# Layer-0 edge messages: VectorE's order of work, gathers by four tiles, and the sum of message parts

## The reference

```
x0, x1 = up0[snd], up1[snd]
m0e = tpw[:, 0] * x0 * sh0 + tpw[:, 3] * einsum('ecx,ex->ec', x1, sh1) * inv3
m1e = tpw[:, 1] * x0 * sh1 + tpw[:, 2] * x1 * sh0
msg0, msg1 = segment_sum(m0e, rcv), segment_sum(m1e, rcv)
```

## Time and profile before

| what | value |
|---|---|
| median of 3 runs | 7333.85 us (7325.06 to 7340.73) |
| span of the profiled execution | 7330.0 us |
| its gathers of layer 0, first start to last start | 236.3 to 2475.7 us |
| busy: DVE, POOL, PE, ACT | 5382.1, 5369.7, 2470.3, 2192.0 us |

### The profile page before, as it was taken

One profiled execution on the slowest core, in us unless ns is written; L12 is line 12 of the kernel. 1 busy time (PEld: TensorE's weight loads), 2 busy tenths in 40 slices (PEclk: granted clock), 3 DMA queues, 4 the chain that ended last, 5 costly groups with the idle time before them and its releaser, 6 DMA issues. The chain is left out here.

```text
span 7330.0 us, 60701 instructions
## 1 busy us (share of the span) xinstructions
PE 2470.3 (34%) x11329; PEld 1690.9 (23%) x11329; DVE 5382.1 (73%) x9193; ACT 2192.0 (30%) x4860; POOL 5369.7 (73%) x5323
## 2 busy tenths in 40 slices
PE   4688888888888577000000000005100000000000
PEld 3455555555555366000000000004100000000000
DVE  7789888888888668667666666774566766666678
ACT  2678778777777453000000000001000000000001
POOL 4677777777777655777777777767777777777775
PEclk8899989999999899555555555558655555555555
DMA  7666666666666548666666666664566667666677
GB/s 227 191 192 198 190 190 190 190 189 189 189 190 188 153 137 214 204 215 216 210 222 209 220 211 216 216 192 106 166 212 214 217 208 224 208 219 213 213 224 238
DMA packets 793610, 1467.69 MB, mean 200 GB/s; under 512 B 187561, under 2 KB 524078, under 8 KB 793004
## 3 DMA queue, kind: packets, MB, share of 16 engines
q0 software_dynamic: 250192, 671.13, 33.5%
q1 hardware_dynamic: 543324, 795.56, 32.0%
HBM read 754.20 MB, written 713.36 MB: 200 GB/s over the span
## 5 line engine op out<-in xcount | busy, mean ns | idle before, releaser
L1775 POOL DMA_INDIRECT gb_g<-table,ix_g x3126 | 2967.3, 949 | 954.3 <-issue 949.1
L656 POOL DMA_INDIRECT gb<-table,src x1563 | 1765.6, 1130 | 492.6 <-issue 476.0
L1881 DVE SCALAR_TENSOR_TENSOR gb_g<-gb_g,same_g,wv 128x256 f32<-128x256 f32 x3024 | 1449.1, 479 | 90.4
L1043 PE MATMUL pm<-ident,tl 128*4 128x128 f32 x2 | 0.7, 374 | 3983.8 <-DMA tl<-sums 3983.8
L690 PE MATMUL po<-parts,sel 128*128 128x256 f32 x3930 | 1035.1, 414 | 272.1 <-ACT ost L756 160.1
L1808 ACT ACTIVATE ww<-ee 128x132 f32<-128x132 f32 (+3 forms) x102 | 28.5, 280 | 3601.3 <-DVE ee L1859 3601.3
L1869 DVE TENSOR_TENSOR wv<-gb_g,ww 128x1024 f32<-128x1024 f32 x782 | 954.8, 1221 | 0.0
L1043 PEld LDWEIGHTS pm<-ident,tl 128*4 128x4 f32 x2 | 0.2, 81 | 3984.6 <-DMA tl<-sums 3984.6
L690 PEld LDWEIGHTS po<-parts,sel 128*128 128x128 f32 x3930 | 767.1, 203 | 517.5 <-issue 283.1
L1851 DVE TENSOR_TENSOR ee<-gb_g,held 128x128 f32<-128x128 f32 (+3 forms) x102 | 37.9, 372 | 1064.4 <-DMA gb_g<-table,ix_g 1064.2
L756 ACT ACTIVATE ost<-po 128x1024 f32<-128x1024 f32 x393 | 399.4, 1016 | 313.4 <-PE po L690 313.4
(11 more groups left out here) (291 smaller groups left out, 4253.4 us busy)
## 6 DMA issues: line engine op xcount, KB each, us to landing
sums<-gb_g SPq DMA_DIRECT2D x780, 528.0 KB, 3.4
sums<-ost SPq DMA_DIRECT2D x393, 512.0 KB, 3.4
gb_g<-table,ix_g POOLq DMA_INDIRECT x3126, 3.1
gb<-table,src POOLq DMA_INDIRECT x1563
table<-f SPq DMA_DIRECT2D x48, 520.0 KB, 4.0
x<-in_x SPq DMA_DIRECT2D x50, 256.0 KB, 3.7
at<-in_rbf SPq DMA_DIRECT2D x100, 128.0 KB
hT_d<-hT SPq DMA_DIRECT2D x49, 256.0 KB, 3.3
```

The costliest lines, as they stand in the source:

```text
L656: eng.indirect_dma_start(out=gb[:, g, j, 0:4, :].rearrange("p a c -> p (a c)"), out_offset=None, in_=q.table0[:, :], in_offset=bass.Indire ...
L1775: eng.indirect_dma_start(out=gb[:, p, j, 0:FR], out_offset=None, in_=q.table1[:, :], in_offset=bass.IndirectOffsetOnAxis(ap=ix[:, p, j:j + ...
L1881: ins = eng.scalar_tensor_tensor(rows[:, t0 + t, 0:D], row, same[:, t:t + 1], wv[k % 2][:, j, :], ALU.mult, ALU.add)
```

## The change

VectorE adds the message parts of all four tiles (`BOTH = 4`, L802 has 1024 elements), and TensorE no longer adds any, so that a step has eight matmul records in `sums`. The dot products are formed for four tiles in each step instead of eight in each odd one, and for the step that comes next. VectorE's list in each step becomes: `k2`, `total` of the step before, `msg`, `dot_products` of the next step (768), `y`, `dot_first` (256), `both` (512), `dot_second` (256). Instructions with one operand in PSUM (`k2`, `msg`, `y`, `both`) and those with both in SBUF take turns. GpSimd's wait for room comes before each four gathers, and VectorE waits for four gathers.

```diff
-    BOTH = 3
+    BOTH = 4
...
-        dots = sb(c, "dots", [P, 8, 3, C])
+        dots = sb(c, "dots", [P, 2, 4, 3, C])
...
-        s_g = [Signal(q.sem(f"g{g}"), per=8, inc=16) for g in range(B)]
+        s_g = [Signal(q.sem(f"g{k}"), per=4, inc=16) for k in range(K)]
...
-        dv = Signal(q.sem("dv"), per=K + K // 2 * 3, ahead=1)
+        dv = Signal(q.sem("dv"), per=4 * K, ahead=1)
...
+        half = lambda k: 4 * ((k - 1) % 2)
+        filled = lambda last, k: min(4, max(0, FILLED - half(k))) if last and k > K - 2 else 4
...
-                    for g in range(B):
-                        eng.wait_ge(s_use.sem, s_use.at(i, 2 * g + 2, back=1))
+                    for k in range(1, K + 1):
+                        eng.wait_ge(s_use.sem, s_use.at(i, k, back=1))
                         eng.nop(nofuse=True)
-                        for j in range(FILLED if last and g == B - 1 else 8):
+                        for j in range(filled(last, k)):
...
+                def dot_products(i, k, last):
...
+                    rows, factors = tiles(k)
+                    n = filled(last, k)
+                    if n > 0:
+                        eng.wait_ge(s_g[k - 1].sem, s_g[k - 1].at(i, n))
+                    if k % 2 == 1:
+                        eng.wait_ge(s_sh[group(k)].sem, s_sh[group(k)].at(i))
+                    return eng.tensor_tensor(dots[:, k % 2, :, :, :], rows[:, :, 1:4, :], bc(factors[:, :, 1:4], 3, [P, 4, 3, C]), ALU.mult)
+
+                def dot_first(k):
+                    return eng.tensor_tensor(tiles(k)[0][:, :, 4, :], dots[:, k % 2, :, 0, :], dots[:, k % 2, :, 1, :], ALU.add)
+
+                def dot_second(k):
+                    qd = tiles(k)[0][:, :, 4, :]
+                    return eng.tensor_tensor(qd, qd, dots[:, k % 2, :, 2, :], ALU.add)
...
+                        eng.wait_ge(s_ts.sem, s_ts.at(i, k))
+                        eng.tensor_tensor(w[:, :, 1, :], x0, w[:, :, 1, :], ALU.mult).then_inc(dv.sem, 1)
                         total(i, k - 1)
...
                         eng.wait_ge(s_sum.sem, s_sum.at(i, k - 4))
...
+                        eng.wait_ge(dv.sem, dv.at(i, n + 1))
                         eng.tensor_tensor(msg[:, b, :, 1:4, :], bc(w[:, :, 1, :], 2, [P, 4, 3, C]), s1, ALU.mult)
...
+                        if ahead:
+                            dot_products(i + up, j, last).then_inc(dv.sem, 1)
+                        eng.tensor_tensor(tmp[:, b, :, 1:4, :], x1, bc(w[:, :, 2, :], 2, [P, 4, 3, C]), ALU.mult)
+                        if ahead:
+                            eng.wait_ge(dv.sem, dv.at(i, n + 2))
+                            dot_first(j).then_inc(dv.sem, 1)
+                        eng.wait_ge(dv.sem, dv.at(i, n))
+                        eng.tensor_tensor(both, rows[:, :, 0::4, :], w[:, :, 0::3, :], ALU.mult).then_inc(s_use.sem, 1)
+                        if ahead:
+                            eng.wait_ge(dv.sem, dv.at(i, n + 3))
+                            dot_second(j).then_inc(dv.sem, 1)
```

More of the change, by code:

```diff
@@ L651, in body @@
                 def body(i, last):
-                    for g in range(B):
-                        eng.wait_ge(s_use.sem, s_use.at(i, 2 * g + 2, back=1))
+                    for k in range(1, K + 1):
+                        eng.wait_ge(s_use.sem, s_use.at(i, k, back=1))
                         eng.nop(nofuse=True)
-                        for j in range(FILLED if last and g == B - 1 else 8):
-                            eng.indirect_dma_start(out=gb[:, g, j, 0:4, :].rearrange("p a c -> p (a c)"), out_offset=None,
+                        for j in range(filled(last, k)):
+                            eng.indirect_dma_start(out=gb[:, group(k), half(k) + j, 0:4, :].rearrange("p a c -> p (a c)"), out_offset=None,
                                                    in_=q.table0[:, :],
-                                                   in_offset=bass.IndirectOffsetOnAxis(ap=q.src[:, (i * B + g) * 8 + j:(i * B + g) * 8 + j + 1], axis=0)).then_inc(s_g[g].sem, 16)
+                                                   in_offset=bass.IndirectOffsetOnAxis(ap=q.src[:, (i * K + k - 1) * 4 + j:(i * K + k - 1) * 4 + j + 1], axis=0)).then_inc(s_g[k - 1].sem, 16)
                 for i in range(SB):
@@ L788, in _ @@
                 eng.memset(m23[:, :, :], 0.0).then_inc(s_wz, 1)
-                eng.sem_inc(dv.sem, dv.base)
+                eng.sem_inc(dv.sem, dv.base - 3)
                 eng.tensor_scalar(behind2[:, :], q.lastpos[:, :], -2.0, None, ALU.mult).then_inc(s_bh, 1)
@@ L802, in total, with tiles @@
                     eng.tensor_tensor(m, m, tmp[:, k % 4, 0:BOTH, :, :], ALU.add).then_inc(s_msg.sem, 1)
-                def body(i, last):
[L805 to L811, removed]
-                    for k in range(1, K + 1):
[L814 to L819, removed]
+                def tiles(k):
+                    return gb[:, group(k), half(k):half(k) + 4, :, :], sh[:, group(k), half(k):half(k) + 4, :]
@@ new lines, in dot_second @@
+                def dot_second(k):
+                    qd = tiles(k)[0][:, :, 4, :]
+                    return eng.tensor_tensor(qd, qd, dots[:, k % 2, :, 2, :], ALU.add)
+                def body(i, last):
+                    for k in range(1, K + 1):
+                        b, n = k % 4, 4 * (k - 1)
+                        ahead = not (last and k == K)
+                        j, up = (k + 1, 0) if k < K else (1, 1)
+                        rows, factors = tiles(k)
+                        x0, x1 = rows[:, :, 0, :], rows[:, :, 1:4, :]
+                        s1 = bc(factors[:, :, 1:4], 3, [P, 4, 3, C])
@@ L820, in body @@
                         w = pt[k % 2][:, :, :].rearrange("p t (a c) -> p t a c", c=C)
-                        y = tmp[:, b, :, :, :]
-                        qd = gb[:, g, :, 4, :]
                         both = parts[:, b:b + 5:4, :, 0, :].rearrange("p s t c -> p t s c")
[L824 to L827, removed]
+                        eng.wait_ge(s_ts.sem, s_ts.at(i, k))
@@ L834, in body @@
-                        eng.wait_ge(s_sum.sem, s_sum.at(i, k - 4))
[L835 to L839, removed]
-                        eng.tensor_tensor(msg[:, b, :, 1:4, :], bc(w[:, :, 1, :], 2, [P, 4, 3, C]), s1, ALU.mult)
@@ L841, in body @@
-                        eng.wait_ge(dv.sem, dv.at(i, k6))
-                        eng.tensor_tensor(both, gb[:, g, ts, 0::4, :], w[:, :, 0::3, :], ALU.mult).then_inc(s_use.sem, 1)
-                    assert n == dv.per
+                        eng.wait_ge(s_sum.sem, s_sum.at(i, k - 4))
+                        eng.wait_ge(dv.sem, dv.at(i, n + 1))
+                        eng.tensor_tensor(msg[:, b, :, 1:4, :], bc(w[:, :, 1, :], 2, [P, 4, 3, C]), s1, ALU.mult)
+                        if ahead:
+                            dot_products(i + up, j, last).then_inc(dv.sem, 1)
@@ L844, in _ @@
+                dot_products(0, 1, False).then_inc(dv.sem, 1)
+                eng.wait_ge(dv.sem, dv.at(0, -2))
+                dot_first(1).then_inc(dv.sem, 1)
+                eng.wait_ge(dv.sem, dv.at(0, -1))
+                dot_second(1).then_inc(dv.sem, 1)
                 over(eng, body)
```

## The result

Four executions of the changed kernel took 7206.83, 7268.46, 7344.3 and 7344.56 us (median 7306.38), the kernel before 7337.29. Its executions fall apart by their mean granted clock: 0.683, 0.667, 0.647 and 0.651. The ratio is taken from the first two, since the two at the lower clock are over 1.5% above the fastest: 0.9876 (0.9837 to 0.9914), some 91 us less; by the median of all four it is 31 us less. The profiled execution is one at 0.647, span 7342.4 us, and must be read as such.

What follows compares the result with a forecast made beforehand. The prediction took GpSimd's issue of gathers, 2242 us, to bound the kernel. VectorE's new pace of 2109 us plus 37 us of waits for ScalarE made 2146, 96 less, so 7238 us, range 7196 to 7345.

Steps and rivals of the forecast that it cites:

- The bound before: Layer 0's edges: GpSimd's issue of 1563 gathers, some held by VectorE instructions with two SBUF operands, fills the 2242 us stage.
- VectorE's own sum: VectorE's list in layer 0's edges: 5.33 us a step, 10.66 against 10.09 for two steps, 112 us more work.
- The pattern: Gathers beside VectorE's new list: four a step of 5.38 us, one held 0.38 us by `dot_products`; 2109 us in all.
- safe side: Dead heat of `total` and a gather: a late `k2` delays `total`, so the gather is first and not held.
- Rival 1: `total` starts before its gather and holds it, 1.09 us more every step; about 7485 us, slower; chance 0.13.
- mean gather: GpSimd's gathers in the stage: forecast to average near 1.04 us, mostly one long gather in four.
- forecast waits of GpSimd for room: GpSimd's gaps between gathers: forecast to be partly waits for `s_use`, room in `gb`; no size given.
- now and then: Short hold of a gather behind `dot_products`, expected only occasionally on top of 6.10 us a step if `total` holds gathers.
- The waits for ScalarE: VectorE waiting for ScalarE in the stage: taken as 37 us added to the time, bounds 0 and 100.
- no wait: Case in which VectorE never waits for ScalarE in the stage: 7201 us.
- rival 3: ScalarE late as the clock falls more often with fewer records; 100 us of waits, gain 30, 7305 us; chance 0.12.
- GpSimd's release: Alternating VectorE order leaves one held gather in four, so VectorE, not GpSimd, sets the pace: 2109 us against 2242.

Runs made afterwards that it cites:

- e7: Changed kernel, fourth tile's `sums` matmul done twice, `total`, `dot_products` and `dot_first` reading their second operand from PSUM; second chip: 8699.52 us, ratio 1.021.
- e11: Changed kernel, fourth tile's `sums` matmul done twice, `k2` made for three of four tiles; third chip: 7526.7 us, ratio 1.0272.
- e10: Changed kernel with the fourth tile's `sums` matmul done twice (ten records a step), third chip: 7229.69 us, ratio 0.9867.
- e1: Changed kernel unchanged, run again on the first chip: 7197.11 to 7344.06 us, ratio 0.9855 from the first three executions.
- e3: Changed kernel with the fourth tile's `sums` matmul done twice (ten records a step), first chip: 7229.63 us, ratio 0.9867.
- e9: Kernel before with `BOTH = 4` and the fourth tile's matmul done twice, old VectorE order, third chip: 7234.19 us, ratio 0.9878.
- e2: Changed kernel with `BOTH = 3`, so TensorE adds the fourth tile's parts again, first chip: 7239.24 us, ratio 0.9878.
- e4: Kernel before with `BOTH = 4` alone, old order, gathers by eight, first chip: 7334.62 us, one execution at 7160.26.
- e12: Kernel before with `BOTH = 4`, ten records and GpSimd's wait for room before each four gathers, third chip: 7225.06 us, ratio 0.9862.
- e5: Kernel before with `BOTH = 4` and the fourth tile's matmul done twice, old VectorE order, second chip: 8704.45 us, ratio 1.0205.

## Why the prediction came out as it did

**The bound before: right.** Held gathers set GpSimd's time: 410 of 1563 are held before by one of the four kinds, 195 by L827, 165 by L802 and 50 by the two additions. e7 shows the cause (both operands in SBUF), e11 the price. The inference on the Trainium skill's page "SBUF — State Buffer", section Who interferes with whom, that `tensor_tensor` does not stall descriptor generation, does not hold for these gathers: 1.98 us against 0.95 in e11 and e10. That the other rule there is the right one, two SBUF inputs contend with a GpSimd instruction that reads SBUF, fits e7; no run shows which read of the gather it is that waits.

**VectorE's own sum: right.** Forecast 5.33 us a step, 2089 in all, and 2109 with the 0.05 us that `total` loses to the gather in every step. In the profiled execution after, `total` runs from 263.6 to 2505.0 us, 2241 us. Of the 150 us of waits for ScalarE in the page's row, 17 lie before the first `total`, so 134 are within: 2108 are left. In e10 it runs from 264.0 to 2400.2, 2136 us, of which 32 are waits: 2104.

**The pattern: right where nobody is late, and as narrow as feared.** Four gathers a step, one held, 5.37 us. It has a second form that the prediction did not see. It said that a late `k2` moves `total` to the safe side of its gather. It moves `total` onto the next one (here `k2` had waited 1.45 us, until 747.85):

```profile
748.19 1.22 DVE L804 TENSOR_TENSOR parts<-parts 128x1024 f32<-128x1024 f32 x1
749.16 1.07 POOL L658 DMA_INDIRECT gb<-table,src  x1 [0.30 <-issue]
```

In the execution profiled after, `total` holds a gather in 135 of the 138 steps in which `k2` waited, and in e10 in 41 of 41, but in none of e10's other steps. These holds cost VectorE nothing, as it waits for no gather.

Rival 1 was nearer than the forecast allowed. With `total` and a gather recorded within 0.02 us of each other, who wins is not settled by the record: `total` held the gather in 29 of 239 such steps after, 27 of 257 in e1, 11 of 313 in e3, and in none of 329 in e10. It does so in spells, step after step 5.33 apart:

```profile
1183.52 2.05 POOL L658 DMA_INDIRECT gb<-table,src  x1 [0.30 <-issue]
1183.53 1.22 DVE L804 TENSOR_TENSOR parts<-parts 128x1024 f32<-128x1024 f32 x1
```

Only three gathers fit into such a step (2.05, 1.43 and 0.95 us), so GpSimd's lead shrinks, but the spells are short enough that VectorE never waits for it. These holds and those behind a late `k2` are why the mean gather is 1120 ns after and 1057 in e10, where 1.04 us was forecast. The forecast waits of GpSimd for room did not come either: its gaps are issue alone, 480.7 us after and 475.9 in e10. What ends a spell, and why e10 has none, stays open.

In e11, rival 1's condition is met in nearly every step, and `total` holds 386 gathers. In 210 steps it starts 0.04 to 0.06 us before the gather and holds it each time. Its price was given as 7485 and measured as 7527: besides `total`, `dot_products` holds a gather of the same step (1.43 at 1006.07 in e11's order of time), which I had called "now and then".

**The waits for ScalarE: the term that was mis-sized.** I took 37 us between bounds of 0 and 100. From the first `total` to the last it is 32 us in e10, with ten records and a steady clock. But it is 134 in the profiled execution at 0.647 and 118 in e1's of 7332 us, both over the upper bound. The best execution of e1, 7197, is 134 us faster than that one, somewhat more than all its waits; so by this estimate it waited hardly at all, and it lies where the prediction put "no wait" (7201). The term is thus not one number: near 0 in some executions of the same kernel and over 100 in others. That the ratio of 0.9876 lies by the forecast's 0.987 is in part luck, because it is the middle of an execution of 7207 and one of 7268. The median of all four, 7306, lands on rival 3 (7305). The mechanism of rival 3 was named, with the clock falling more often as records get fewer; its bound was too small, and its chance (0.12) as well, since five of ten executions of the changed kernel went that way. How much one kernel's executions scatter was also missed: the prediction took 15 us for what can be told from no change. How it goes, in the profiled execution (busy row of a low stretch, then order of time):

```profile
735.00:745.00 10.00, 7.36 (x23) 4.19 (x24) 10.00 (x15) 6.00 (x14) 7.87 (x8) 0.65 0.55 165
```

```profile
738.89 3.75 PE L692 MATMUL po<-parts,sel 128*128 128x256 f32 x8 [2.18 <-ACT ost L758]
...
744.58 2.08 PE L682 MATMUL pt<-m,r 64*128 64x256 f32 x8
...
747.85 0.43 DVE L837 TENSOR_TENSOR pt<-gb,pt 128x256 f32<-128x256 f32 x1 [1.45 <-ACT pt L752]
```

TensorE pauses 2.18 us, then eight records of `sums` take 3.75 us instead of the 1.97 at full clock (704.42 in the same trace), `paths` 2.08 instead of 1.14, and `k2` waits 1.45 us. With VectorE the bound, each such wait counts in full. Such slow spells are in e10 too (3.63 us for `sums` at 1006.94), but fewer: the clock in the stretch is 0.97 there. That fewer records bring this about is shown by e3 and e10 against e1: two more records, which give VectorE nothing, and no execution near 0.65 in ten, where the changed kernel has five in ten. With `BOTH = 4` in the old order it is the same: five of six near 0.65 in e4, none of ten in e9 and e12. On the first and third chips no execution of any kernel with ten records fell below 0.678. Why some executions of the same kernel keep the clock and others do not stays open.

**What the change as a whole is worth: my credit went to the wrong part.** The prediction credited the alternating order with GpSimd's release. That release comes as well from `BOTH = 4` in the old order (e9: 7234, with ten records), and from the new order with `BOTH = 3` (e2: 7239); both together with ten records give 7230. In the old kernel, L802 began 0.06 to 0.08 us before a gather in 165 of 392 steps (308.04 in the earlier trace rows) and cost it 0.76 us each time. In e9, where nobody is late, a gather starts 0.16 us ahead of `total` instead (1009.78 and 1009.94) and is free. In none of the three kernels does VectorE then wait more than 1.9 us for gathers. That the shift of phase is the whole reason is argued for e9 and e2, and tested by itself only in e11. The three gains do not add up, because behind the holds stands VectorE's own sum and then the chain through ScalarE. In the old order, which has fewer and longer instructions, that sum is the smaller one (10.63 against 10.66 us for two steps).

## What to carry to other kernels

Where one engine's instructions block another's at their start, work out the phases over one period from rows before counting busy time: here 0.07 us of phase was worth 297 us, and an edit with less work was slower. Before taking matmuls off TensorE, look at the granted clock: with a fifth fewer records in one group, executions of one kernel lay 147 us apart. And run the parts of a change by themselves, since two parts can each buy the same gain.

## What was not expected of the hardware

- The same program with the same input ran at a mean clock of 0.683 in 7197 us or at 0.647 in 7344 us on one chip; with two more matmul records a step all ten executions, on two chips, lay between 7223 and 7276.
- A gather recorded up to 0.02 us before a VectorE instruction with two SBUF operands mostly goes free and delays that instruction a little (`total` 1.25 instead of 1.22 us), but in up to an eighth of such steps it is held (2.05 us). One that starts 0.04 us or more behind was held to the instruction's end in every case counted (210 of 210 in e11), unless it starts in the instruction's last 0.13 us.
- On one chip the kernel before took 8522 us, 16% more. No trace of it was kept there; in e5, on the same chip, ScalarE waited up to 8.4 us at a time for what is read as the stores, while a free gather kept its 0.95 us (e7's median is 946 ns).
